# Order of the value matmuls and the side jobs in the second layer's attention of a two-layer transformer kernel

## The chip, the cores and the metric

The kernel runs on one core of one Trainium2 chip. The metric is the time of one execution on the device, in microseconds (us). TensorE, VectorE, ScalarE, GpSimd and SyncE are called PE, DVE, ACT, POOL and SP in the rows, as the profile does.

## What is computed

The input is x, four batches of 1024 tokens of 128 numbers (float32). Two layers are applied, each an attention and a mixture of experts, with a layer norm and a scale and shift ahead of each part. The change touches only the attention of the second layer, layer 1 in the code. It has 16 heads of 8 numbers, in three kinds:

```
outs.append(_sdpa(q[:, :N1], k[:, :N1], v[:, :N1], 1.0 / math.sqrt(HD)))             # 6 heads: softmax(q k)
outs.append(_hyp_attn(q[:, N1:N1 + N2], k[:, N1:N1 + N2], v[:, N1:N1 + N2], curvature))  # 4 heads: hyperbolic
outs.append(_sdpa(qn, kn, v[:, N1 + N2:], math.sqrt(HD)))                            # 6 heads: q and k normalised
```

All are causal. The score of a hyperbolic head is 1 / (eps + arccosh(argument)), where the argument comes from the product of query and key.

## The kernel before

**Batches.** The program goes through the four batches one after the other: layer 0 attention and experts, then layer 1 attention; the experts of layer 1 of a batch run together with the start of the next batch. The engines run separate programs that are tied by semaphores, and a barrier stands between batches.

**Units and steps.** The 16 heads are four units of four heads. Units 0, 1 and 2 of layer 1 are the plain heads (called standard), unit 3 is the hyperbolic one. A unit is cut into 12 steps (`STEPS`): two query chunks of 512 columns, and for each the key blocks of 128 that are not wholly masked. A step has 512, 384, 256 or 128 query columns. Steps 0 to 3 have 512, 384, 256, 128; steps 4 to 8 have 512; steps 9 to 11 have 384, 256, 128.

**Positions.** In layer 1 a loop over positions p (0 to 37) sets the order. With s = p modulo 12, TensorE's program (`tensor_program`, `attention`) does in position p:

1. `scores(p + 1)`: four score matmuls (line 699) in two pairs, one pair into each two-bank buffer. Up to three side jobs are put between them.
2. `values(p)`: the exponentials of step p (tile pr, four heads) against the values vt (line 745). The four heads write 32 partitions each of one PSUM bank, by `tile_position=(0, 32 * j)`, which is 32 columns of the array each. A float32 matmul shows as two instructions, so two heads are x4 in the rows and four heads x8.
3. from p = 6 on `hyp_values(p - 6)`: the value matmuls of two hyperbolic heads (line 772), in the same manner.
4. the side jobs that are left.
5. from p = 3 on `hyp_scores(p - 3)`: two score matmuls (line 715) of hyperbolic heads.

**Side jobs.** Before its own softmax a unit needs the largest score of each query. These are found from a second computation of the scores, cut into pieces: a piece is a matmul of up to 512 columns (line 626), with a mask matmul (line 629) on the diagonal, and a VectorE reduction of its bank (line 1279). The pieces are the side jobs, together with the transposes of the maxima (`max`), of finished outputs (`turn`, line 660) and some work for the next batch. The planner `side_plan` deals them to positions. Side jobs have two PSUM banks, 6 and 7, in turn, and job g waits until VectorE is done with job g - 2:

```
elif g >= 2:
    pe.wait_ge(a.side_out, g - 1)
```

I number the TensorE jobs of a position e0, e1, e2, ... The first three are taken by `scores`; e3 and e4 are the two that the change moves. The number of TensorE jobs in a position, where it is 4 or more, is 11, 5, 10, 9, 8, 6, 9, 7, 6, 4 in positions 0 to 9 and 9, 6, 4, 8, 5, 6, 5, 4, 4 in positions 13 to 21. Positions 10 to 12 and from 22 on have at most three.

**The other engines.** ScalarE does in a position the exponentials of the standard step (line 1008) and, for three hyperbolic half steps in different stages, seven activations: `hyp_exp` (997), `hyp_score` (986, 989, 992), `hyp_root` (980, 981). VectorE does `hyp_arg` (lines 1339, 1344), then the first half of the position's side list, then `hyp_shift` (line 1352), on which ScalarE's next `hyp_exp` depends, then the other half:

```
first = (len(SIDE[l, more][p]) + 1) // 2 if l and k >= 0 else 99
```

(k is p - 3, so this holds from position 3 on; the list counts entries for VectorE alone, such as `maxima`.) GpSimd adds two tiles in `L1616` and masks diagonals. The maxima of the hyperbolic unit go through ScalarE in `hyp_max` (line 967 is its first instruction), at the end of positions 1 and 5. The maxima of unit 1 are formed after position 9 and those of unit 2 after position 21; each goes by a DMA of SP (`send_maxima`) into the query operand before the unit's scores.

Of the kernel before, what the change touches and what calls it, by code (L numbers as in the profile page):

```python
# [53 lines left out]
def diagonals(g):  # L54

    return g // NS * sum(x[4] for x in STEPS) + sum(x[4] for x in STEPS[:g % NS])
# [7 lines left out]
def is_hyp(l, u):  # L64
    return l == 1 and u == HYP_UNIT
# [12 lines left out]
def slot(l, u):  # L78

    return (0, 1, 0, 2)[u] if l else u % SLOTS  # L80
# [16 lines left out]
def nth(l, u):  # L97

    return ((0, 1, 2, 3), (HYP_UNIT, 1, 2))[l].index(u)
# [89 lines left out]
def side_bank(g):  # L189
    return (6, 7)[g % 2]  # L190
# [47 lines left out]
def adaln_kernel(nc, ins, out):  # L238
    with ExitStack() as ctx:
# [105 lines left out]
        def xT(b):  # L345
            return xTs[:, b % 2, :]

        def hT(b):
            return hTs[:, b % 2, :]
# [185 lines left out]
        def chunk(t, c):  # L535
            return t[:, c * CH:(c + 1) * CH]


        def tensor_program(pe, b):
# [18 lines left out]
            def attention(l):  # L558
# [4 lines left out]
                def count(kind, what):  # L563
                    return side_count(l, more, kind, what)
# [44 lines left out]
                def side_job(kind, g, what):  # L609

                    if g == 0:
                        pe.wait_ge(a.v if l == 0 else a.proj_used, NT if l == 0 else 4)
                        if l == 0 and more:
                            pe.wait_ge(fs[1].gates, NC)
                    elif g >= 2:
                        pe.wait_ge(a.side_out, g - 1)
                    bank = side_bank(g)
                    if kind == "piece":
                        u, j, p = what
                        qb, k0, wd, _ = PIECES[p]  # L620
                        if (j, p) == (0, 0):
                            pe.wait_ge(a.ops[u], OPS_HYP if is_hyp(l, u) else OPS)
                        k = K_HYP if is_hyp(l, u) else PAIRS
                        o = ps[:, bank, 0:wd]
                        diag = k0 + wd == (qb + 1) * P
                        mm = pe.matmul(o, qop[0:k, slot(l, u), j, qb * P:(qb + 1) * P],  # L626
                                       kop[0:k, slot(l, u), j, k0:k0 + wd], start=True, stop=not diag)
                        if diag:
                            mm = pe.matmul(o[:, wd - P:wd], identb[:], maskqk[:], start=False, stop=True)  # L629
                    elif kind == "max":  # L630
                        pe.wait_ge(a.nmp, MAXES[l].index(what) + 1)
                        if is_hyp(l, what[0]):
                            mm = pe.transpose(ps[0:32, bank, 0:P], nm[:, nth(l, HYP_UNIT) % 2, :], w["ident"][:])
                        else:
                            mm = pe.matmul(ps[0:96, bank, 0:P], nmp[:], identb[:], start=True, stop=True)
                    elif kind == "out":
                        c = what[0]
                        pe.wait_ge(fs[1].x, c + 1)
                        for t in range(4):
                            mm = pe.transpose(ps[:, bank, t * P:(t + 1) * P],  # L640
                                              xT(b - 1)[:, c * CH + t * P:c * CH + (t + 1) * P], w["ident"][:])
                    elif kind == "xT":
                        c = what[0]
                        pe.wait_ge(x_in, 16)
                        for t in range(4):
                            mm = pe.transpose(ps[:, bank, t * P:(t + 1) * P], xin[:, 4 * c + t, :], w["ident"][:])
                    elif kind == "hT":
                        c = what[0]
                        pe.wait_ge(ln_norm[0], 4 * (c + 1))
                        for t in range(4):  # L650
                            mm = pe.transpose(ps[:, bank, t * P:(t + 1) * P], xin[:, 4 * c + t, :], w["ident"][:])
                    elif kind == "kp":
                        c = what[0]
                        pe.wait_ge(a.side_out, count("hT", (c,)))
                        mm = pe.matmul(ps[:, bank, :], w["wk"][:], chunk(hT(b + 1), c), start=True, stop=True)
                    else:
                        i = what[0]
                        pe.wait_ge(a.o_out, i + 1)
                        for t in range(4):
                            mm = pe.transpose(ps[:, bank, t * P:(t + 1) * P], osb[:, i % 2, t * P:(t + 1) * P],  # L660
                                              w["ident"][:])
                    mm.then_inc(a.side, 1)
# [58 lines left out]
                def out_before(u, c):  # L721

                    same = [i for i, (_, v, d) in enumerate(OUTS[l]) if is_hyp(l, v) == is_hyp(l, u)
                            and (v, d) < (u, c)]
                    return max(same, default=-1) + 1

                def values(g, extra):
                    u, s = divmod(g, NS)
                    c, kb, q0, wd, diag = STEPS[s]
                    o0 = q0 - c * CH  # L730
                    last = kb == 4 * c + 3
                    if diag:
                        pe.wait_ge(a.cut, diagonals(g + 1))
                    else:
                        pe.wait_ge(a.exps, 2 * (g + 1))
                    if kb == 0:
                        if g == 0:
                            pe.wait_ge(a.v, NT if l == 0 else 2)
                        else:
                            pe.wait_ge(a.o_out, out_before(u, c))  # L740
                            if l == 0:
                                pe.wait_ge(a.s_out, NC * u + c)
                    for j in range(4):
                        h = 4 * u + j
                        mm = pe.matmul(ps[32 * j:32 * j + 32, 4, o0:o0 + wd], vt[:, kb, 32 * h:32 * h + 32],  # L745
                                       pr[:, g % 3, j, o0:o0 + wd], start=kb == 0, stop=last,
                                       tile_position=(0, 32 * j))
                        if l and j == 3:
                            mm.then_inc(a.pv, 1)
                        if l and j % 2 and extra:  # L750
                            side_job(*extra.pop(0))
                    if l == 0:
                        for j in range(4):
                            mm = pe.matmul(ps[32 * j:32 * j + 32, 5, o0:o0 + wd], ones32[:],  # L754
                                           pr[:, g % 3, j, o0:o0 + wd], start=kb == 0, stop=last,
                                           tile_position=(0, 32 * j))
                        mm.then_inc(a.pv, 1)
# [18 lines left out]
                def jobs_at(p):  # L776
                    return [x for x in SIDE[l, more][p] if x[1] is not None]
# [9 lines left out]
                for p in range(POSITIONS[l] + 1):  # L787
                    extra = jobs_at(p)
                    if p + 1 < steps:
                        scores(p + 1, extra)  # L790
                    if p < steps:
                        values(p, extra)
                    if l and 0 <= p - HYP_AT - 3 < HYP_HALVES:
                        hyp_values(p - HYP_AT - 3)
                    for x in extra:
                        side_job(*x)
                    if l and 0 <= p - HYP_AT < HYP_HALVES:
                        hyp_scores(p - HYP_AT)
# [1111 lines left out]
```

## Time and profile before

| what | value |
|---|---|
| median of 3 runs | 2942.42 us (2936.65 to 2943.5) |
| the profiled execution | 2944.73 us, its span 2942.8 us |
| PE busy | 2303.2 us, 78% |
| DVE busy | 1553.3 us, 53% |
| ACT busy | 1378.9 us, 47% |
| POOL busy | 657.2 us, 22% |
| mean granted TensorE clock | 0.814 |
| value matmuls, line 745 | 2688 instructions, 442.8 us busy, both layers |

The busy shares are means over stages with different limits. The granted clock is a share of TensorE's full speed of 2.4 GHz: 0.5 stands for the lower level, 1.2 GHz. The attention of layer 1 takes about 276 us of each batch, in the first batch from about 407 to 683 us of the span.

### The profile page before, as it was taken

What the parts mean: (1) busy time and instruction counts of PE and PEld (TensorE: products, weight loads), DVE (VectorE), ACT (ScalarE), POOL (GpSimd) and SP (SyncE); (2) the same over time, 40 slices, a digit from 0 to 9 for tenths busy, and PEclk for the clock granted to TensorE, in tenths of its full rate; (3) what the DMA queues carried; (4) which work ended last, traced back from release to release, by engine and by line L of the source; (5) the groups of instructions that cost most, each with busy time, mean ns of one, the idle gap of its engine ahead of it and who ended that gap; (6) DMA issues with size and microseconds to landing.
All of it is one profiled execution on the core that took longest, in us unless ns stands there. A gap on an engine that the chain in (4) does not pass through costs nothing. (4 is left out here: it accounts for less than half of the span.)

```text
span 2942.8 us, 30130 instructions
## 1 busy us (share of the span) xinstructions
PE 2303.2 (78%) x10649; PEld 866.6 (29%) x10649; DVE 1553.3 (53%) x3429; ACT 1378.9 (47%) x1963; POOL 657.2 (22%) x639
## 2 busy tenths in 40 slices
PE   3799847777999884777798987667789998477789
PEld 1222321223433341122343234121334223212134
DVE  2553446675456354666455526467545634466642
ACT  1145315893134531788224452288622453248932
POOL 1012101332321210233241120033223111013324
PEclk8599866678999885777799987578689998667789
DMA  5100220001400022000330003110032002200012
GB/s 142 40 18 2 73 71 30 17 1 50 128 23 18 16 66 77 27 6 1 95 98 25 2 22 87 50 32 1 12 112 70 18 1 73 67 21 30 1 34 90
DMA packets 67750, 128.32 MB, mean 44 GB/s; under 512 B 11300, under 2 KB 24740, under 8 KB 62980
## 3 DMA queue, kind: packets, MB, share of 16 engines
q1 hardware_dynamic: 67600, 126.40, 14.8%
q8 instruction: 84, 1.38, 0.2%
q14 instruction: 66, 0.54, 0.1%
HBM read 109.99 MB, written 15.20 MB: 43 GB/s over the span
## 5 line engine op out<-in xcount | busy, mean ns | idle before, releaser
L1279 DVE TENSOR_REDUCE mx<-ps 128x1 f32<-128x512 f32 (+3 forms) x1248 | 644.0, 552 | 562.3 <-PE ps L629 468.6
L1008 ACT ACTIVATE pr<-ps 128x1024 f32<-128x1024 f32 (+3 forms) x672 | 515.9, 804 | 537.0 <-PE ps L699 534.4
L626 PE MATMUL ps<-kop,qop 72*128 72x512 bf16 (+6 forms) x1248 | 441.3, 372 | 158.2 <-DVE mx L1279 90.1
L699 PE MATMUL ps<-qop,kop 75*128 75x512 bf16 (+7 forms) x1344 | 409.8, 370 | 160.2 <-DMA kop<-parts_scratch 56.5
L745 PE MATMUL ps<-pr,vt 128*32 128x512 f32 (+3 forms) x2688 | 442.8, 590 | 5.2 <-POOL pr L1563 4.6
L1563 POOL TENSOR_SCALAR_AFFINE_SELECT pr<-pr 128x512 f32<-128x512 f32 x224 | 145.9, 651 | 987.5 <-ACT pr L1008 986.1
L1063 ACT ACTIVATE pr<-ps 128x512 f32<-128x512 f32 x224 | 133.8, 597 | 405.1 <-PE ps L851 316.4
L626 PEld LDWEIGHTS ps<-kop,qop 72*128 72x128 bf16 (+1 forms) x1248 | 124.7, 101 | 608.0 <-DVE mx L1279 342.8
L861 PE MATMUL ps<-pr,w_down 128*128 128x512 f32 x384 | 211.5, 638 | 69.6 <-POOL pr L1554 48.8
L699 PEld LDWEIGHTS ps<-qop,kop 75*128 75x128 bf16 (+1 forms) x1344 | 123.4, 105 | 380.3 <-ACT pr L1008 122.4
L848 PE MATMUL ps<-hT,w_gate 128*128 128x512 f32 x384 | 205.5, 618 | 0.0
L629 PE MATMUL ps<-maskqk,identb 128*128 128x128 bf16 x832 | 200.2, 247 | 0.0
L754 PE MATMUL ps<-pr,ones 128*32 128x512 f32 (+3 forms) x1536 | 166.6, 506 | 0.0
L1329 DVE COPY osb<-ps 128x512 f32<-128x512 f32 x64 | 44.0, 688 | 203.0 <-PE ps L754 176.2
L1554 POOL TENSOR_TENSOR pr<-on,wb 128x512 f32<-128x512 f32 x84 | 106.0, 1264 | 179.6 <-DVE on L1501 129.6
L851 PE MATMUL ps<-hT,w_up 128*128 128x512 f32 x256 | 134.2, 607 | 0.0
L1339 DVE TENSOR_SCALAR wb<-ps 128x1024 f32<-128x1024 f32 (+3 forms) x96 | 91.5, 953 | 72.2 <-PE ps L715 68.0
L1501 DVE TENSOR_TENSOR on<-pr,ps 128x512 f32<-128x512 f32 x84 | 57.3, 682 | 106.9 <-ACT pr L1063 102.3
L861 PEld LDWEIGHTS ps<-pr,w_down 128*128 128x128 f32 x384 | 71.3, 201 | 139.9 <-POOL pr L1554 58.2
L745 PEld LDWEIGHTS ps<-pr,vt 128*32 128x32 f32 x2688 | 69.5, 117 | 133.5 <-issue 108.1
L1616 POOL TENSOR_TENSOR wb<-wb 128x1024 f32<-128x1024 f32 (+3 forms) x36 | 70.9, 1969 | 169.1 <-ACT wb L981 169.1
L715 PE MATMUL ps<-qop,kop 84*128 84x512 bf16 (+3 forms) x192 | 61.8, 414 | 54.4 <-ACT pr L1008 54.4
(298 smaller groups left out, 3012.3 us busy)
## 6 DMA issues: line engine op xcount, KB each, us to landing
wb<-gates_scratch SPq DMA_DIRECT2D x192, 256.0 KB, 3.3
qop<-parts_scratch SPq DMA_DIRECT2D x96, 192.0 KB
kop<-parts_scratch SPq DMA_DIRECT2D x96, 192.0 KB
on<-hmax_scratch SPq DMA_DIRECT2D x8, 1024.0 KB, 5.5
parts_scratch<-on SPq DMA_DIRECT2D x24, 256.0 KB, 3.4
parts_scratch<-wb SPq DMA_DIRECT2D x24, 256.0 KB, 2.9
xin<-in_x SPq DMA_DIRECT2D x4, 512.0 KB, 4.5
on<-in_cos SPq DMA_DIRECT2D x4, 512.0 KB, 3.8
```

The lines of the kernel that those rows point to most:

```text
L626: mm = pe.matmul(o, qop[0:k, slot(l, u), j, qb * P:(qb + 1) * P], kop[0:k, slot(l, u), j, k0:k0 + wd], start=True, stop=not diag)
L629: mm = pe.matmul(o[:, wd - P:wd], identb[:], maskqk[:], start=False, stop=True)
L699: mm = pe.matmul(o, kop[0:k, slot(l, u), 2 * pair + j, kb * P:(kb + 1) * P], qop[0:k, slot(l, u), 2 * pair + j, q0:q0 + wd], start=True, s ...
L745: mm = pe.matmul(ps[32 * j:32 * j + 32, 4, o0:o0 + wd], vt[:, kb, 32 * h:32 * h + 32], pr[:, g % 3, j, o0:o0 + wd], start=kb == 0, stop=la ...
L754: mm = pe.matmul(ps[32 * j:32 * j + 32, 5, o0:o0 + wd], ones32[:], pr[:, g % 3, j, o0:o0 + wd], start=kb == 0, stop=last, tile_position=(0 ...
L848: mm = pe.matmul(ps[:, f.gate_banks[i % R], :], wt, h, start=True, stop=True)
L851: mm = pe.matmul(ps[:, 4 + i % 2, :], wt, h, start=True, stop=True)
L861: pe.matmul(ps[:, c, :], wt, fh[:, i % 3, :], start=i < NC, stop=i == f.last[c]).then_inc(g.down, 1)
L1008: nc.scalar.activation(pr[:, g % 3, 2 * pair:2 * pair + 2, o0:o0 + wd], ps[:, bank:bank + 2, o0:o0 + wd], ACT.Exp).then_inc(a.exps, 1)
L1063: nc.scalar.activation(fa[:, i % 3, :], ps[:, f.gate_banks[i % R], :], fn).then_inc(g.act, 1)
L1279: ins_ = nc.vector.tensor_reduce(mx[:, nth(l, u) % 2, j, qb, col % 2:col % 2 + 1], ps[:, bank, 0:wd], AX.X, ALU.max, negate=True)
L1563: nc.gpsimd.affine_select(past, past, [[0, 4], [1, P]], ALU.is_ge, 0.0, base=0, channel_multiplier=-1).then_inc(at[l].cut, 1)
```

## The change

In `values`, the two lines that put a side job behind the second and the fourth head are gone. The value matmuls of the four heads stand in a row, and the jobs that stood among them are taken by the loop over `extra` behind `hyp_values`, which is unchanged.

```diff
--- before.py
+++ after.py
@@ -747,8 +747,6 @@
                                        tile_position=(0, 32 * j))
                         if l and j == 3:
                             mm.then_inc(a.pv, 1)
-                        if l and j % 2 and extra:
-                            side_job(*extra.pop(0))
                     if l == 0:
                         for j in range(4):
                             mm = pe.matmul(ps[32 * j:32 * j + 32, 5, o0:o0 + wd], ones32[:],
```

The instructions of the other engines, and their order, are the same as before. Lines behind the edit have numbers smaller by two in the changed kernel (772 becomes 770).

TensorE in position 0 of layer 1, from the last score matmul on, before. L745 is `values`, L626 with L629 a piece:

```order
L699 MATMUL ps<-qop,kop 128x384
L626 MATMUL ps<-kop,qop 128x128
L629 MATMUL ps<-maskqk,identb 128x128
L745 MATMUL ps<-pr,vt 32x512 x2
L626 MATMUL ps<-kop,qop 128x128
L629 MATMUL ps<-maskqk,identb 128x128
L745 MATMUL ps<-pr,vt 32x512 x2
L626 MATMUL ps<-kop,qop 128x256
L629 MATMUL ps<-maskqk,identb 128x128
```

The same place with the change:

```order
L699 MATMUL ps<-qop,kop 128x384
L626 MATMUL ps<-kop,qop 128x128
L629 MATMUL ps<-maskqk,identb 128x128
L745 MATMUL ps<-pr,vt 32x512 x4
L626 MATMUL ps<-kop,qop 128x128
L629 MATMUL ps<-maskqk,identb 128x128
L626 MATMUL ps<-kop,qop 128x256
L629 MATMUL ps<-maskqk,identb 128x128
```

The piece e3 now stands behind all four heads, and e4 follows it at once.

TensorE in position 13, from e2 on, before. L772 is `hyp_values`:

```order
L626 MATMUL ps<-kop,qop 128x128
L629 MATMUL ps<-maskqk,identb 128x128
L745 MATMUL ps<-pr,vt 32x384 x2
L626 MATMUL ps<-kop,qop 128x128
L629 MATMUL ps<-maskqk,identb 128x128
L745 MATMUL ps<-pr,vt 32x384 x2
L626 MATMUL ps<-kop,qop 128x256
L629 MATMUL ps<-maskqk,identb 128x128
L772 MATMUL ps<-rsb,vt 32x128 x2
L626 MATMUL ps<-kop,qop 128x256
L629 MATMUL ps<-maskqk,identb 128x128
```

The same place with the change, where L770 is `hyp_values`:

```order
L626 MATMUL ps<-kop,qop 128x128
L629 MATMUL ps<-maskqk,identb 128x128
L745 MATMUL ps<-pr,vt 32x384 x4
L770 MATMUL ps<-rsb,vt 32x128 x2
L626 MATMUL ps<-kop,qop 128x128
L629 MATMUL ps<-maskqk,identb 128x128
L626 MATMUL ps<-kop,qop 128x256
L629 MATMUL ps<-maskqk,identb 128x128
L626 MATMUL ps<-kop,qop 128x256
L629 MATMUL ps<-maskqk,identb 128x128
```

Here e3 and e4 have moved behind `hyp_values` as well.

## Rows read from the trace of the kernel before

**Rows 1.** Windows of the first batch's layer 1: busy us by engine, PEclk.

```profile
434.30:493.90 59.60, 45.75 (x155) 11.83 (x155) 33.78 (x65) 19.62 (x35) 6.60 (x5) 0.59 0.08 29
453.70:467.70 14.00, 13.21 (x51) 4.28 (x52) 8.65 (x18) 3.27 (x5) 1.27 (x2) 0.50 0.20 64
493.90:533.00 39.10, 30.51 (x142) 8.79 (x142) 29.10 (x56) 35.63 (x55) 13.52 (x16) 0.85 0.08 29
582.80:660.00 77.20, 55.08 (x255) 15.65 (x255) 57.67 (x116) 74.87 (x102) 28.11 (x25) 0.81 0.00 1
```

**Rows 2.** Timeline of PE: value matmuls of two heads, and of four.

```profile
588.19 1.05 PE L745 MATMUL ps<-pr,vt 128*32 128x512 f32 x4
589.18 0.28 PE L626 MATMUL ps<-kop,qop 72*128 72x256 bf16 x1
...
670.39 1.07 PE L745 MATMUL ps<-pr,vt 128*32 128x512 f32 x8
```

**Rows 3.** Waits of the whole run: us in total, times, longest.

```profile
PE ps L626 <- DVE mx L1279: 90.1, 201, 1.2
...
ACT nr L967 <- DVE nr L1238: 79.1, 8, 14.3
```

**Rows 4.** Timeline of ACT, first batch: three ends of idle time.

```profile
450.66 0.22 ACT L967 ACTIVATE nr<-nr 128x16 f32<-128x16 f32 x1 [14.30 <-DVE nr L1238]
...
552.95 1.06 ACT L997 ACTIVATE wb<-wb 128x1024 f32<-128x1024 f32 x1 [3.32 <-DVE wb L1352]
...
568.63 1.06 ACT L980 ACTIVATE xn<-xn 128x1024 f32<-128x1024 f32 x1 [1.91 <-DVE xn L1344]
```

**Rows 5.** Timeline of PE, positions 0 and 1: heads 2 and 3.

```profile
437.84 1.92 PE L745 MATMUL ps<-pr,vt 128*32 128x512 f32 x4
439.69 0.40 PE L626 MATMUL ps<-kop,qop 84*128 84x256 bf16 x1
...
447.13 1.50 PE L745 MATMUL ps<-pr,vt 128*32 128x384 f32 x4
```

**Rows 6.** Timeline of PE: position 2's heads 2 and 3; e5 of positions 2 to 4.

```profile
457.41 1.07 PE L745 MATMUL ps<-pr,vt 128*32 128x256 f32 x4
...
458.60 0.32 PE L626 MATMUL ps<-kop,qop 84*128 84x128 bf16 x1
...
465.59 0.42 PE L626 MATMUL ps<-kop,qop 84*128 84x256 bf16 x1
...
477.50 0.42 PE L626 MATMUL ps<-kop,qop 84*128 84x384 bf16 x1
```

**Rows 7.** Timeline of DVE: e3 of positions 2 to 4; position 5 from its shift.

```profile
457.52 0.69 DVE L1279 TENSOR_REDUCE mx<-ps 128x1 f32<-128x512 f32 x1 [0.85 <-PE ps L626]
...
464.82 0.42 DVE L1279 TENSOR_REDUCE mx<-ps 128x1 f32<-128x256 f32 x1 [0.32 <-PE ps L629]
...
475.35 0.56 DVE L1279 TENSOR_REDUCE mx<-ps 128x1 f32<-128x384 f32 x1 [1.83 <-PE ps L629]
...
486.98 1.22 DVE L1352 TENSOR_TENSOR hT<-hT,on 128x1024 f32<-128x1024 f32 x1
488.54 1.29 DVE L1279 TENSOR_REDUCE mx<-ps 128x1 f32<-128x512 f32 x2 [0.34 <-PE ps L629]
```

**Rows 8.** Timeline of PE: positions 9, 13 (two rows) and 14.

```profile
524.93 0.81 PE L772 MATMUL ps<-wb,vt 128*32 128x384 f32 x4
...
549.39 1.49 PE L745 MATMUL ps<-pr,vt 128*32 128x384 f32 x4
...
551.25 0.64 PE L772 MATMUL ps<-rsb,vt 128*32 128x128 f32 x4
...
560.54 1.07 PE L745 MATMUL ps<-pr,vt 128*32 128x256 f32 x4
```

**Rows 9.** Timeline of DVE, position 16: the shift.

```profile
579.66 3.10 DVE L1352 TENSOR_TENSOR xn<-xn,on 128x1024 f32<-128x1024 f32 x1
```

**Rows 10.** Timeline of POOL, position 16.

```profile
579.33 2.35 POOL L1616 TENSOR_TENSOR rsb<-rsb,wb 128x1024 f32<-128x1024 f32 x1 [6.11 <-ACT rsb L981]
```

## Prediction

> **What bounds the kernel now.** I read the windows of the first batch's layer 1 first. They show which engine is full in which stretch, and so where time saved on TensorE is worth anything. From 434.3 to 493.9 us (positions 0 to 5) TensorE is busy 45.75 of 59.6 us and ScalarE only 19.62; from 582.8 to 660.0 (positions 17 and later) ScalarE is busy 74.87 of 77.2 us [rows 1]. So the first stretch runs at TensorE's pace, and in the last one a faster TensorE buys nothing. From 493.9 to 533.0 (positions 6 to 11) ScalarE has 35.63 of 39.1 us, nearly full.
>
> Next the value matmuls. Two heads of 512 columns take 1.05 us, with 0.99 us from their start to the next instruction; four heads in a row take 1.07 us, not 2.1 [rows 2]. The four heads use different columns of the array and run side by side. Two pairs with a job between them pay twice. That is the time the change can take out: the second pair of each position that has four or more side jobs, 19 positions a batch.
>
> Then the waits. TensorE's side jobs wait for VectorE's reductions, 90.1 us in 201 waits, and ScalarE waits 79.1 us in all, in 8 waits (two a batch) for the hyperbolic maxima [rows 3]. The longest in the first batch is 14.30 us, before 450.66 [rows 4]. It ends when the last pieces of position 1 are reduced: whatever TensorE saves before them moves the rest of the layer forward. ScalarE's other idle times in this batch that TensorE can shorten stand in positions 13 and 14: 3.32 and 1.91 us.
>
> **The change, part by part.** No instruction is added or removed; e3 and e4 move. I take the first batch and multiply by four, since the 79.1 us of the waits for the maxima are close to four times its own two.
>
> *Positions 0 and 1: gain 3.3 us.* The second pair of position 0 costs 439.69 - 437.84 = 1.85 us, that of position 1 1.50 less the same 0.07 of overlap, 1.43 [rows 5]. Four heads in a row cost what the first pair costs, by rows 2. After the values the jobs go on as before, only earlier. Both second pairs stand ahead of the last reductions, so the full 3.28 counts.
>
> *Positions 2 to 5: gain 2.9 us.* There the reductions limit it, since with e3 and e4 side by side e5 must wait until e3 is reduced. Position 2: e3's reduction ends at 457.52 + 0.69 = 458.21, and e5 began at 458.60, so the gain is 0.39 at e5 [rows 6, 7]; the second pair is worth 1.00 at most (1.07 less overlap); pieces of 128 columns follow, quick to reduce, and I take 0.6. Position 3: 464.82 + 0.42 = 465.24 against 465.59, 0.35; I take 0.45. Position 4: 475.91 against 477.50, 1.59; two more pieces follow at the reductions' pace of 0.56 each, and I take 1.45. Position 5: `hyp_shift` stays where it was, since e3 is still the last job before it and starts as before. It ends at 488.20, and e4 was reduced from 488.54: 0.34. Sum 2.84. The low bound is 0.39 + 0.35 + (1.59 - 0.56) + 0.34 = 2.1, the high one the pairs themselves, 1.00 + 0.45 + 1.85 + 1.85 = 5.2 (for positions 4 and 5, of 512 columns, I take position 0's).
>
> *Positions 6 to 9: loss 0.8 us.* Now `hyp_values` stands ahead of e3 and e4. In position 6, e4 is the last job before the shift; it gains one pair and loses one `hyp_values` of the same cost, nothing; I book 0.1 lost. In position 7 e3 is the last, and comes later by one pair, 0.98; see below why I book only 0.1. In position 9 e3 is the last piece but none before unit 1's maxima, and nothing may start on unit 1 until these are sent. It comes later by the 0.81 us of `hyp_values` less 0.07 [rows 8], part of which VectorE's shift covered; I book 0.6. In position 8 the shift does not depend on e3 or e4. TensorE's own saving in these positions meets a full ScalarE, so I cost it at nothing; that cover is gone where ScalarE idles, and there is some of that in the other batches.
>
> *Positions 13 and 14: gain 1.7 us.* In 13, e4 is again the last before the shift. It gains the pair, 1.49 - 0.07 = 1.42, and pays `hyp_values` of 128 columns, 0.57: 0.85 net, and ScalarE waits there 3.32 us on that shift [rows 4, 8]. In 14 the shift is untouched, but `hyp_scores` come earlier by the pair, 1.00, less the wait for e3's reduction ahead of the last job, 0.15; ScalarE waits 1.91 us for their result. I take 0.85.
>
> *Positions 15 to 21: loss 0.2 us.* In 16, e3 is the last before the shift and comes about 1.05 us later. But there the shift took 3.10 us, where others of its shape take 1.22 [rows 7, 9]. It began 0.33 us after GpSimd's addition, which ran until 579.33 + 2.35 = 581.68, and ended at 582.76 [rows 10]. Started a microsecond later it still ends about there: nothing lost. Position 7 has the same pattern. Without this cover positions 7 and 16 would lose 2.0 us more a batch, 8 in all, and the time would be 2923. The Trainium skill (SBUF — State Buffer, "Who interferes with whom") says that a VectorE instruction with two SBUF inputs is blocked for the whole length of a GpSimd instruction that reads SBUF. The 3.10 us agree. In 21, unit 2's maxima come later by part of a `hyp_values`; behind the same kind of cover, 0.2.
>
> *Sum.* 3.28 + 2.84 + 1.70 - 0.8 - 0.2 = 6.8 us a batch, 27 in all. The profiled execution took 2944.7, which gives 2917.5; the median of the runs is 2.3 lower, so 2915. With positions 2 to 5 at 2.1 and positions 7 and 16 uncovered it is 4.1 a batch, 2926; with positions 2 to 5 at 5.2 it is 9.2, 2906.
>
> **The rivals.**
>
> *The reductions set the pace everywhere.* The Trainium skill (TensorEngine Tiling (Array Packing), "PSUM Bottleneck") warns that a faster, packed TensorE may leave the PSUM evacuation as the bottleneck. Here that would mean: only positions 0 and 1 gain, 3.3 less 1.0 lost, 9 us in all, 2933. For it speaks position 5, where 0.34 of 1.85 is left. Against it, VectorE is busy only 33.78 of 59.6 us there [rows 1]. The sum by my rows is 2915, by that rule 2933. Chance 0.10.
>
> *The clock is lost.* Positions 0 to 5 have a mean granted clock of 0.59, which is 18% of 59.6 us, 10.7 us, at 2.4 GHz and the rest at 1.2 [rows 1]. If the denser order brings less of the higher level, TensorE's work of these 10.7 us takes up to twice as long; some 7 of it would be on the path, which takes the whole gain: 2942. For it speaks that 13.21 busy us of 14 were not enough for the higher level between 453.7 and 467.7 (0.50). Against it: no work is taken out. Chance 0.06.
>
> *The clock is won.* The same stretch at 2.4 GHz would take TensorE half of 13.2 us, and VectorE's 8.65 would bind it: up to 5 us a batch more, 2895. Chance 0.08.
>
> *Slower: the shift is held up.* e3 and e4 stand behind `hyp_values` in 13 positions (6 to 9, 13 to 21). If in each of them VectorE's shift had to wait for them, ScalarE's full stretch would grow by a `hyp_values` each time, 13 x 1.0 = 13 us a batch against a gain of 6.1 in positions 0 to 5: 7 lost a batch, 28 in all, 2970. It decides from about seven such positions on. Against it speaks the rule for the first half of the list: only in positions 6, 7, 13 and 16, with lists of 7 to 9 entries, does that half reach e3 or e4; in the others it holds three at most. For it: a late e3 holds e5 and with it `hyp_scores`, and the full ScalarE has little slack. Chance 0.10.
>
> **How the numbers follow.** My forecast has 0.66. Two runs of this kernel differ by some 0.2%, so 0.3%, 9 us, is what a measurement can tell from no change. Faster by more than that: the forecast, the clock won and half of the first rival, 0.79. Within: the other half and the clock lost, 0.11. Slower: 0.10. The range goes from 2894, the clock won, to 2939, behind the first rival; it leaves out the slower case, the lost clock and a few in a hundred beyond the low end.
>
> **What would show it.** The value matmuls of positions 0 to 21 stand as x8 of 1.07 us (about 1.9 at the lower clock), none as x4. The first batch's wait before line 967 falls from 14.30 to about 11.0. The stretch from the first piece of position 0 to the second `hyp_max` is shorter by about 6 us, and the stretch from position 17 on has the same length, with ScalarE full. The shifts of positions 7 and 16 end as late after GpSimd's addition as before. It is wrong if the wait at 552.95 grows, if the x8 groups take twice 1.05, or if positions 15 to 22 grow by more than a microsecond.

## The result, and the profile after

The changed kernel takes 2927.27 us (median of 4 runs, 2924.84 to 2929.63), the kernel before on the same chip 2942.96 (4 runs, 2936.65 to 2946.84). The ratio is 0.9949, with an interval of 0.9929 to 0.9968. A second comparison, with more runs, stands among the experiments: 0.997 [0.9953, 0.9987]. So the change makes the kernel faster by 0.3 to 0.5% (the two intervals reach from 0.1 to 0.7%). That is inside the range, on the side that was forecast, and smaller: 16 us by the first comparison and 7 by the second, where 27 were forecast.

The page of the changed kernel, its busy times and the group of value matmuls (busy us, mean ns of one):

```profile
PE 2286.9 (78%) x10649; PEld 872.5 (30%) x10649; DVE 1541.9 (53%) x3429; ACT 1379.5 (47%) x1963; POOL 656.4 (22%) x639
...
L745 PE MATMUL ps<-pr,vt 128*32 128x512 f32 (+3 forms) x2688 | 361.7, 617 | 5.2 <-POOL pr L1561 4.7
```

The value matmuls take 361.7 us where they took 442.8, 81 less. All of TensorE is busy only 16 us less: its other instructions took 65 us longer, and its mean granted clock went from 0.814 to 0.790.

The wait for the hyperbolic maxima, which the first term rested on, fell as forecast. A wait of the changed kernel (us in total, times, longest), then ScalarE's timeline in the first batch:

```profile
ACT nr L965 <- DVE nr L1236: 65.8, 8, 11.7
```

```profile
447.48 0.22 ACT L965 ACTIVATE nr<-nr 128x16 f32<-128x16 f32 x1 [10.77 <-DVE nr L1236]
...
508.64 0.84 ACT L995 ACTIVATE rsb<-rsb 128x768 f32<-128x768 f32 x1 [2.39 <-DVE rsb L1350]
...
551.16 1.06 ACT L995 ACTIVATE wb<-wb 128x1024 f32<-128x1024 f32 x1 [2.64 <-DVE wb L1350]
...
565.91 1.06 ACT L978 ACTIVATE xn<-xn 128x1024 f32<-128x1024 f32 x1 [0.97 <-DVE xn L1342]
...
580.12 1.06 ACT L995 ACTIVATE xn<-xn 128x1024 f32<-128x1024 f32 x1 [1.76 <-DVE xn L1350]
```

Against [rows 4]: 14.30 became 10.77 (11.0 forecast), 3.32 became 2.64 and 1.91 became 0.97. But the second line is new. ScalarE waits 2.39 us for the shift of position 7, where the kernel before had:

```profile
512.98 0.84 ACT L997 ACTIVATE rsb<-rsb 128x768 f32<-128x768 f32 x1 [0.92 <-DVE rsb L1352]
...
582.80 1.06 ACT L997 ACTIVATE xn<-xn 128x1024 f32<-128x1024 f32 x1 [1.72 <-DVE xn L1352]
```

**Where the time went.** I cut each batch's layer 1 at marks on ScalarE: the first instruction of each `hyp_max`, then the score activation (line 984, 986 before) of positions 9, 11, 16, 18, 22 and 28. Lengths in us; where one number stands, it is the mean of the four batches' gains.

| stretch | before, batches 1 to 4 | changed | mean gain | forecast |
|---|---|---|---|---|
| first piece of position 0 to first `hyp_max` | 16.37, 15.44, 16.37, 16.38 | 12.84, 13.77, 12.78, 12.95 | 3.06 | 3.28 |
| to the second `hyp_max` (positions 2 to 5) | 39.83, 38.44, 39.79, 39.80 | 37.21, 37.22, 37.21, 37.20 | 2.25 | 2.84 |
| to position 9 (positions 6 to 8) | 29.57, 31.90, 29.58, 29.58 | 31.04, 31.63, 31.13, 30.90 | -1.02 | -0.2 |
| 9 to 11 | 9.84, 10.34, 9.83, 9.83 | 12.89, 10.59, 10.54, 12.90 | -1.77 | -0.6 |
| 11 to 16 | 43.54, 43.29, 43.39, 42.14 | 42.09, 41.05, 41.42, 42.00 | 1.45 | 1.7 |
| 16 to 18 | 18.96, 19.16, 19.15, 18.18 | 19.20, 19.86, 19.86, 19.20 | -0.67 | -0.2, to 21 |
| 18 to 22 | 33.6, 35.4, 35.4, 34.4 | 33.6, 33.6, 33.6, 33.6 | 1.1 | 0 |

From position 22 to 28 every batch has the same length as before to 0.01 us. The rows add to 4.4 us a batch, 18 in all; the profiled span is shorter by 2942.8 - 2927.9 = 14.9, so some 3 us were lost elsewhere. Most of the missing time is in positions 6 to 11: 0.8 booked as lost, 2.8 measured. The windows of the changed kernel for the stretches of [rows 1] (busy us by engine, then PEclk, DMA share, GB/s), then for positions 9 to 11 of the four batches:

```profile
434.64:488.18 53.54, 39.21 (x156) 11.10 (x156) 33.67 (x65) 19.70 (x35) 6.62 (x5) 0.56 0.10 32
488.18:532.00 43.82, 35.55 (x142) 10.22 (x142) 27.51 (x56) 36.00 (x54) 13.09 (x16) 0.62 0.07 25
580.20:657.50 77.30, 57.33 (x255) 17.56 (x255) 58.29 (x116) 74.82 (x102) 28.46 (x25) 0.69 0.00 1
...
515.73:528.62 12.89, 9.90 (x50) 3.29 (x48) 9.39 (x22) 9.41 (x19) 4.09 (x7) 0.63 0.01 2
1221.99:1232.58 10.59, 6.54 (x47) 2.49 (x47) 9.19 (x22) 9.32 (x19) 4.12 (x7) 0.91 0.00 1
1928.64:1939.18 10.54, 6.58 (x47) 2.49 (x47) 9.14 (x22) 9.31 (x19) 4.11 (x7) 0.91 0.00 1
2635.55:2648.45 12.90, 9.95 (x50) 3.24 (x48) 9.39 (x22) 9.42 (x20) 4.10 (x7) 0.63 0.00 1
```

The first stretch lost 6.5 us of TensorE work and 6.1 us of length. The second, of positions 6 to 11, grew from 39.1 to 43.8 and its clock fell from 0.85 to 0.62. The last kept its length with ScalarE full, although its clock fell too, from 0.81 to 0.69. The last four rows are one order of instructions in four batches: two batches had a clock of 0.91 and took 10.5 us, two had 0.63 and took 12.9. The kernel before had 0.95 and 9.84 in the first batch:

```profile
520.06:529.90 9.84, 6.60 (x47) 2.27 (x44) 8.43 (x20) 9.21 (x19) 4.13 (x7) 0.95 0.01 3
```

**Position 7, where the new wait is.** TensorE before and after:

```profile
509.05 1.05 PE L745 MATMUL ps<-pr,vt 128*32 128x512 f32 x4
510.04 0.23 PE L626 MATMUL ps<-kop,qop 72*128 72x128 bf16 x1
...
510.25 1.05 PE L745 MATMUL ps<-pr,vt 128*32 128x512 f32 x4
```

```profile
503.56 1.94 PE L745 MATMUL ps<-pr,vt 128*32 128x512 f32 x8
505.28 1.92 PE L770 MATMUL ps<-xn,vt 128*32 128x512 f32 x4
507.13 0.23 PE L626 MATMUL ps<-kop,qop 72*128 72x128 bf16 x1
```

VectorE in the changed kernel:

```profile
507.45 0.29 DVE L1277 TENSOR_REDUCE mx<-ps 128x1 f32<-128x128 f32 x1 [3.10 <-PE ps L629]
507.66 0.95 DVE L1350 TENSOR_TENSOR rsb<-rsb,on 128x768 f32<-128x768 f32 x1
```

e3 used to come 1 us behind the start of the values. Now it stands behind `values` and `hyp_values`, and both take 1.9 us each at the lower clock: 3.57 us. VectorE waits 3.10 us for it, and the shift that ScalarE needs stands behind that reduction in VectorE's list.

In batches 1, 3 and 4 this one wait is all that positions 6 to 8 lost: they grew by 1.47, 1.55 and 1.32 us, and ScalarE's wait for this shift grew from 0.92 or 0.93 to 2.39, 2.48 and 2.24.

Two things are mixed here, the order and the clock. They call for these theories: **order** (a job that the first half of VectorE's list reaches holds the shift, so it is cured by moving e3 and e4 or by shortening the list), **clock alone** (the lower clock came by itself and the order is innocent), and **too little work on the array** (grouping empties TensorE, and that is why the clock falls).

### The profile page after: what moved, and what is told of

It reads as the page before. It is cut to its first block and busy times, and to the rows that moved or that the text cites. A ratio compares the mean times of both kernels' runs of the same rounds, so it can differ in the third digit from the quotient of the medians.

```text
span 2927.9 us, 30130 instructions
## 1 busy us (share of the span) xinstructions
PE 2286.9 (78%) x10649; PEld 872.5 (30%) x10649; DVE 1541.9 (53%) x3429; ACT 1379.5 (47%) x1963; POOL 656.4 (22%) x639
## 5 line engine op out<-in xcount | busy, mean ns | idle before, releaser
L626 PE MATMUL ps<-kop,qop 72*128 72x512 bf16 (+6 forms) x1248 | 457.8, 389 | 160.2 <-DVE mx L1277 93.7
L699 PE MATMUL ps<-qop,kop 75*128 75x512 bf16 (+7 forms) x1344 | 428.2, 384 | 150.9 <-DMA kop<-parts_scratch 56.3
L745 PE MATMUL ps<-pr,vt 128*32 128x512 f32 (+3 forms) x2688 | 361.7, 617 | 5.2 <-POOL pr L1561 4.7
L626 PEld LDWEIGHTS ps<-kop,qop 72*128 72x128 bf16 (+1 forms) x1248 | 126.1, 103 | 568.2 <-DVE mx L1277 319.7
L629 PE MATMUL ps<-maskqk,identb 128*128 128x128 bf16 x832 | 203.7, 252 | 0.0
L846 PEld LDWEIGHTS ps<-hT,w_gate 128*128 128x128 f32 x384 | 75.1, 199 | 91.8 <-issue 75.0
```

The source lines that it names most:

```text
L699: mm = pe.matmul(o, kop[0:k, slot(l, u), 2 * pair + j, kb * P:(kb + 1) * P], qop[0:k, slot(l, u), 2 * pair + j, q0:q0 + wd], start=True, s ...
L846: mm = pe.matmul(ps[:, f.gate_banks[i % R], :], wt, h, start=True, stop=True)
```

## Experiments

Each kernel is the changed one with the edit shown, unless said otherwise. Each of the three sets ran on a chip of its own, so I compare by the ratio to the kernel before on the same chip. That kernel had 2940.99, 2941.84 and 2939.37 us there, from 23 to 29 runs.

### Set 1: where the gain is made, and e3 and e4 moved back ahead

Grouped in positions 0 to 5 only:

```diff
+                        if l and g >= 6 and j % 2 and extra:
+                            side_job(*extra.pop(0))
```

> The four value matmuls are grouped only in positions 0 to 5 of layer 1; from position 6 on e3 and e4 stand among them as in the kernel before. Theory A (the lower granted clock in positions 6 to 12 comes from the grouping there, and ate most of the gain): the gain of positions 0 to 5 stays, 6.1 us a batch, 24 in all, and the granted clock between position 6 and 12 is again about 0.85; time 2918 to 2921. Theory B (the clock level there is chance, or follows from the earlier positions): the clock stays at 0.62 there and the time is 2925 to 2930, like the changed kernel.

Measured: 2932.68 us, 0.9971 [0.9947, 0.9996]. Faster, by 8 us where the forecast's terms for 0 to 5 come to 24. Neither theory's range holds the time. Its profiled execution took 2956.46 us, 24 above its own median, so its trace can only hint. Positions 0 to 5 took 49.9 to 51.0 us there, as in the changed kernel. Positions 6 to 8, where the jobs stand as before, took 30.9, 30.0, 30.0 and 30.2 us at clocks of 0.70 to 0.75; three batches of the kernel before had 29.6 at 0.83. So a part of the loss behind position 5 may come from what the grouping of positions 0 to 5 leaves behind. That is not shown.

Grouped from position 6 on only (the same lines with `g < 6`):

> The complement: grouped only from position 6 on. Theory A: the gain of positions 0 to 5 is gone and the loss of positions 6 to 12 (4 us in the first batch) stands against some 3 us gained in positions 13 to 19: time 2942 to 2950, clock in positions 6 to 12 about 0.62. Theory B: clock there back at 0.85 and time 2935 to 2939.

Measured: 2936.06, 0.9988 [0.997, 1.0005], not told from no change, and within theory B's range. But the clock in positions 6 to 8 was 0.62 to 0.72, so theory B's clock did not come with it. Gains and losses from position 6 on about cancel. Its first stretch, which is ungrouped as before, took 16.1, 13.2, 13.3 and 12.9 us in the four batches, at clocks of 0.61, 0.85, 0.84 and 0.87. Grouped, the same stretch took 12.95 us at 0.63 in the changed kernel's fourth batch, and 11.6 at 0.79 in two batches of its second trace (changed_again). So the gain depends on the clock: about 3.4 us at the lower one, and some 1.3 to 1.7 at the higher one.

e3 and e4 ahead of `hyp_values`, in all positions:

```diff
+                    for x in extra[:2]:
+                        side_job(*x)
+                    extra = extra[2:]
                     if l and 0 <= p - HYP_AT - 3 < HYP_HALVES:
                         hyp_values(p - HYP_AT - 3)
```

> Grouped everywhere, but e3 and e4 stand behind the four value matmuls and ahead of the hyperbolic ones. Theory C (the loss in positions 6 to 12 comes from e3 and e4 waiting behind the hyperbolic value matmuls, which delays VectorE's shift): the loss goes, time 2912 to 2918. Theory A: the clock stays at about 0.62 in positions 6 to 12 and only the part of the shift waits in positions 7 and 9 comes back, 1 to 2 us a batch: time 2920 to 2925.

Measured: 2903.54 (2886.04 to 2911.74), 0.9881 [0.9853, 0.9908], more than either theory expected. The values stay grouped, and the gain is over twice that of the change.

The same with e3 alone (`extra[:1]`):

> Grouped everywhere; e3 stands behind the four value matmuls, then the hyperbolic ones, then e4. The side jobs break the run of value matmuls once instead of not at all. Theory C: 2912 to 2918. Theory A: if a break between the two groups is what keeps the clock up, the clock in positions 6 to 12 is near 0.85 and the time 2915 to 2920; if the total of column passes side by side matters, it stays near 0.62 and the time is 2920 to 2925.

Measured: 2917.27, 0.9941 [0.9919, 0.9963]. That is clearly less than with both ahead, so e4 counts too. It is the last job before the shift in positions 6 and 13. The interval overlaps that of the changed kernel in set 2.

### Set 2: only where the shift waits, everywhere, and more work on the array

The changed kernel again, as the measure for this set:

> The changed kernel once more, on the same chip as the next three, so that they are compared with it directly. 2922 to 2930 us; in positions 9 to 11 it is slower than before wherever the granted clock there is near 0.65 and not near 1.

Measured: 2934.36 (2922.26 to 2944.15, 12 runs), 0.997 [0.9953, 0.9987], 4 us above the expected range. Its trace repeats the loss: positions 6 to 8 took 31.7, 31.1, 31.7 and 30.9 us, with a wait for the shift of position 7 of 2.1 to 2.5 us in each batch. Positions 9 to 11 took 12.2 to 12.9 us in all four batches, at clocks of 0.60 to 0.63.

e3 and e4 ahead only in the four positions where the first half of VectorE's list reaches them:

```diff
+                    if l and p in (6, 7, 13, 16):
+                        for x in extra[:2]:
+                            side_job(*x)
+                        extra = extra[2:]
```

> e3 and e4 ahead of the hyperbolic value matmuls only in positions 6, 7, 13 and 16, where the first half of VectorE's list reaches them. If VectorE's shift is what they hold up, most of what the kernel with both ahead everywhere gains over the changed one comes back (6 us a batch by the traces): 2904 to 2910. If they hold up something else (the side ring, the maxima, the hyperbolic scores), it stays near 2920 to 2927.

Measured: 2904.5 (2882.99 to 2914.34), 0.9886 [0.9865, 0.9908], as good as moving them in all positions. This bears out the order theory: what costs is that the shift waits, and in four positions. The wait for the shift of position 7 is 0.91 or 0.92 us in every batch of this kernel, as before the change. Positions 6 to 8 of the first batch, changed and shift_only:

```profile
484.69:515.73 31.04, 23.86 (x89) 6.50 (x90) 17.32 (x34) 26.49 (x39) 7.30 (x8) 0.61 0.10 35
```

```profile
482.17:510.53 28.36, 19.80 (x98) 6.25 (x98) 20.25 (x37) 26.50 (x38) 8.93 (x8) 0.79 0.12 38
...
510.53:519.88 9.35, 5.98 (x41) 1.99 (x40) 7.59 (x19) 9.16 (x20) 3.60 (x7) 0.89 0.01 3
1204.55:1216.85 12.30, 8.95 (x48) 3.01 (x47) 9.20 (x21) 9.42 (x20) 4.11 (x7) 0.61 0.00 1
```

The stretch is 2.7 us shorter, and its clock is 0.79, not 0.61. The order works at an equal mean clock too. Positions 6 to 8 took 28.1 us at 0.70 here in the second batch and 27.5 at 0.69 in the fourth batch of list_three (below), but 31.2 at 0.69 in the fourth batch of ahead_13_16, which has the changed order there.

The last two rows are positions 9 to 11, whose order this edit leaves as in the changed kernel: 9.35 us in one batch at 0.89 and 12.30 in the next at 0.61. The order within the stretch does not explain this difference. Nor does its mean clock by itself. Here are two batches of list_three, again with the changed kernel's order in positions 9 to 11:

```profile
510.53:521.23 10.70, 7.77 (x40) 2.45 (x40) 7.09 (x19) 9.30 (x20) 3.79 (x7) 0.57 0.01 2
...
2612.91:2625.80 12.89, 9.96 (x50) 3.33 (x48) 9.39 (x22) 9.42 (x20) 4.08 (x7) 0.63 0.00 1
```

The batch with the lower clock is 2.2 us shorter. Between the same two marks of ScalarE, TensorE has 40 instructions to do there and 50 in the other: it came into the stretch further ahead. And in e3_ahead, where e3 stands ahead in positions 8 and 9 as well, two batches took 9.33 and 9.35 us at 0.59. So what is carried in from position 8 counts beside the clock, and the trace does not part the two.

All side jobs that are left ahead of `hyp_values` (its call moved behind the loop over `extra`):

> Grouped, and all side jobs that are left stand ahead of the hyperbolic value matmuls. If every side job that is earlier helps: a few us below the kernel with both ahead, 2895 to 2903. If the hyperbolic value matmuls between e4 and e5 are useful cover for the reductions: no better, 2903 to 2912.

Measured: 2943.36, 1.0004 [0.9988, 1.002]; the whole gain is gone, and the time lies far above both expected ranges. ScalarE and VectorE of its first batch:

```profile
502.61 0.84 ACT L978 ACTIVATE wb<-wb 128x768 f32<-128x768 f32 x1 [2.08 <-DVE wb L1342]
...
604.73 1.06 ACT L978 ACTIVATE hT<-hT 128x1024 f32<-128x1024 f32 x1 [1.57 <-DVE hT L1342]
```

```profile
500.62 0.96 DVE L1337 TENSOR_SCALAR wb<-ps 128x768 f32<-128x768 f32 x1 [1.90 <-PE ps L715]
```

`hyp_values` (1 to 1.9 us) now stand directly ahead of `hyp_scores` (line 715), and VectorE's `hyp_arg` and then ScalarE wait for these. The second row lies past position 17, where ScalarE had no such wait in the first batch of before and of changed. That `hyp_values` had cost nothing between the side jobs, because TensorE waits for a reduction there anyway, is my reading and not tested. The clock in positions 6 to 8 was 0.50 in this batch, so the clock has a part here as well.

The score matmuls of positions 5 to 11 doubled, 28 more instructions a batch (each writes the same product again):

```diff
+                            for _ in range(2 if l and 6 <= g < 13 else 1):
+                                mm = pe.matmul(o, kop[0:k, slot(l, u), 2 * pair + j, kb * P:(kb + 1) * P],
+                                               qop[0:k, slot(l, u), 2 * pair + j, q0:q0 + wd], start=True, stop=True)
```

> The changed kernel with every score matmul of steps 6 to 12 of layer 1 issued twice, to the same result: 28 more matmuls a batch of up to 512 columns, 0.22 us each at the high clock and 0.43 at the low one. If the low clock in positions 6 to 12 comes from too little work on the array, the clock there goes from 0.62 to 0.85 or more and positions 8 to 11 take 1 to 3 us less a batch: time 2915 to 2927 in spite of the added work. If not: clock as before and 4 to 8 us more a batch, 2940 to 2955.

Measured: 2952.64, 1.0038 [1.0022, 1.0054]. Positions 6 to 8 of the first and the third batch:

```profile
485.95:519.70 33.75, 27.34 (x100) 8.84 (x100) 17.55 (x34) 26.49 (x39) 7.43 (x8) 0.60 0.10 32
1910.07:1940.01 29.94, 22.40 (x100) 7.58 (x100) 17.84 (x34) 26.49 (x38) 8.11 (x8) 0.73 0.11 36
```

With TensorE busy 27.3 us of 33.8 the clock stays at 0.60, and so it does in the second and fourth batch. The third has 0.73, with TensorE busy 22.4 us of 29.9, so less. The added work did not raise the clock, and the theory of too little work on the array has nothing left that speaks for it.

### Set 3: the two pairs of positions apart, and the cure on VectorE

Ahead in positions 6 and 7 only:

> Grouped; e3 and e4 ahead of the hyperbolic value matmuls in positions 6 and 7 only. Theory S (they hold up VectorE's shift where its first half reaches them): positions 6 to 8 take 1.2 us less than before instead of 1.4 more, positions 13 to 16 as in the changed kernel; 2.7 us a batch and, if the low clock in positions 9 to 11 is a consequence of the delay in 6 and 7, up to 3 us more: time 2912 to 2918. If the clock there is independent of it: 2918 to 2924.

Measured: 2912.07, 0.991 [0.9877, 0.9943]. Positions 6 to 8 took 28.1, 30.3, 28.3 and 28.6 us, where the changed kernel had 30.9 to 31.6.

Ahead in positions 13 and 16 only:

> The same in positions 13 and 16 only. Theory S: positions 13 to 16 take 3 us less a batch than in the changed kernel, positions 6 to 11 as there, with the clock in 9 to 11 at 0.63 to 0.73: time 2916 to 2922. The two gains together should make up the 25 to 30 us between the changed kernel and the one with all four positions.

Measured: 2928.7 (2903.82 to 2943.52), 0.9954 [0.9927, 0.9982], above the expected range and not told from the changed kernel. From the score activation of position 14 to that of 18 the batches took 37.60, 37.54, 37.55 and 34.58 us, the changed kernel 37.5 to 37.8 in its first trace (36.5 in two batches of its second). The fourth has a clock of 0.80, the first 0.60:

```profile
548.42:586.02 37.60, 31.13 (x118) 9.32 (x117) 29.49 (x47) 32.92 (x38) 10.87 (x5) 0.60 0.00 1
...
2680.00:2714.58 34.58, 25.09 (x122) 7.57 (x120) 28.88 (x48) 32.77 (x38) 10.81 (x5) 0.80 0.00 1
```

Position 16 shows a threshold. Here are VectorE, GpSimd and ScalarE of its first batch:

```profile
573.48 2.85 DVE L1354 TENSOR_TENSOR xn<-xn,on 128x1024 f32<-128x1024 f32 x1
...
572.90 2.35 POOL L1618 TENSOR_TENSOR rsb<-rsb,wb 128x1024 f32<-128x1024 f32 x1 [6.12 <-ACT rsb L983]
...
576.36 1.06 ACT L999 ACTIVATE xn<-xn 128x1024 f32<-128x1024 f32 x1 [1.71 <-DVE xn L1354]
```

And the same three in shift_only:

```profile
566.67 1.22 DVE L1354 TENSOR_TENSOR xn<-xn,on 128x1024 f32<-128x1024 f32 x1
...
567.40 2.70 POOL L1618 TENSOR_TENSOR rsb<-rsb,wb 128x1024 f32<-128x1024 f32 x1 [6.12 <-ACT rsb L983]
...
569.04 1.06 ACT L999 ACTIVATE xn<-xn 128x1024 f32<-128x1024 f32 x1
```

In ahead_13_16 the shift starts 0.58 us behind GpSimd's addition, takes 2.85 us and ScalarE waits 1.71, as in the kernel before (1.72). In shift_only it starts 0.73 us ahead of the addition, takes 1.22, and ScalarE has no idle time there; the addition takes 2.70 in place of 2.35. An earlier e3 brings nothing until it is early enough to come first. In batches 1 to 3 of ahead_13_16 the shift starts 0.56 to 0.58 us behind the addition; in the fourth it starts 0.73 us ahead, and only there is the stretch 3 us shorter. How close the race can be, other places show: a shift of the same shape that started 0.07 us ahead of an addition took 1.22 us (shift_only, position 6), and one that started 0.07 us behind took 3.36 (list_three, position 13, third batch).

The cure on VectorE: the changed TensorE program, but from position 6 on the shift stands behind at most three entries of its list.

```diff
                     first = (len(SIDE[l, more][p]) + 1) // 2 if l and k >= 0 else 99
+                    if l and k >= 3:
+                        first = min(first, 3)
```

> The changed kernel on TensorE; on VectorE, from position 6 on, at most three side jobs stand ahead of the shift, so that it never waits for e3 or e4. Theory S: the loss goes without any change on TensorE, 2900 to 2915. If the place of e3 and e4 costs through the side ring or the score buffers: 2922 to 2935.

Measured: 2898.66 (2889.49 to 2905.84), 0.9851 [0.9816, 0.9886]. This is just below the range that was expected, and the lowest ratio of all kernels, clearly below before and changed; both_ahead and shift_only have intervals that overlap it. It is the most direct test of the order theory, since TensorE's program stays the changed one. VectorE in position 7:

```profile
501.30 0.94 DVE L1350 TENSOR_TENSOR rsb<-rsb,on 128x768 f32<-128x768 f32 x1
502.73 0.49 DVE L1277 TENSOR_REDUCE mx<-ps 128x1 f32<-128x128 f32 x2 [0.50 <-PE ps L629]
```

The shift starts ahead of e3's reduction, and ScalarE's activation behind it follows at 503.45 with no wait, where the changed kernel had 2.39.

The same VectorE edit on the kernel before:

> The kernel before (pairs with jobs among them) with the same shorter first half on VectorE. Shows what of that gain has nothing to do with the grouping: theory S expects some gain, since e4 of positions 6 and 13 and e3 of 7 and 16 stand ahead of the shift there too, one or two pairs later than they might: 2925 to 2938.

Measured: 2932.32, 0.998 [0.9958, 1.0002]. Without the grouping the short list brings 7 us, with an interval that reaches no change; with it, about 1% or 30 us against the changed kernel (0.9851 against 0.9949 and 0.997). The two edits need each other: the grouping makes e3 and e4 late, the list makes that harmless. The traces show why the list alone brings little. In the first batch of before_list_three ScalarE's wait for the shift of position 7 is gone too, but it waits 1.34 us for `hyp_arg` just ahead, and in positions 16 to 18 2.25 us. With the grouping these waits are 0.62 and 0.59 us.

## Why the prediction was right, and too large

- *Positions 0 and 1, 3.28.* Right: 3.5 us in the three batches whose clock was as in the rows read, 1.67 in the second, which was quicker before (15.44 us, at a clock of 0.69 and not 0.60) and slower after (13.77, at 0.50). Scaling the first batch by four missed that.
- *Positions 2 to 5, 2.84.* Right: 2.6 in three batches, 1.22 in the second. The bounds of 2.1 and 5.2 held for the three. The reductions took most of what four pairs could give, as rows 6 and 7 showed.
- *Positions 6 to 9, a loss of 0.8.* This step failed: 2.8 us lost on average, up to 4.5 (batches 1 and 4). It failed in two terms.
  - Positions 6 to 8 lost 1.3 to 1.6 us in three batches, and all of it is the wait for the shift of position 7, which was booked at 0.1, on the ground that GpSimd's addition covered it. The changed trace shows the shift at 507.66 us, taking 0.95, no longer behind a lock (2.37 us before) but behind e3. The cover was 1.4 us long, and the delay of e3 2.6 (from 0.99 to 3.57 us behind the start of the values). I had priced `values` and `hyp_values` at the 1.0 us of the higher clock, which rows of the same stretch showed at 0.85; at the lower one each costs 1.9.
  - Positions 9 to 11 lost 3.05 us in batches 1 and 4 and 0.25 and 0.71 in the others, where 0.6 was booked because unit 1's maxima come later. That was the wrong wait: in these two traces ScalarE never waits for unit 1's first scores. In the first batch it waits for VectorE's `hyp_arg` (1.15 and 1.16 us) and for a shift (0.96), 3.27 us in all against 0.44 before:

```profile
519.38 0.63 ACT L978 ACTIVATE hT<-hT 128x512 f32<-128x512 f32 x1 [1.15 <-DVE hT L1342]
...
526.80 0.42 ACT L978 ACTIVATE xn<-xn 128x256 f32<-128x256 f32 x1 [1.16 <-DVE xn L1342]
```

- *Positions 13 and 14, 1.7.* Nearly right: ScalarE's two waits fell by 0.68 and 0.94, and the stretch from 11 to 16 by 1.45 on average.
- *Positions 15 to 21, a loss of 0.2.* The cover in position 16 held in the way that was forecast, in three batches of four. In the first the shift began at 578.87 us, as GpSimd's addition ended (576.61 + 2.35 = 578.96), and ScalarE waited 1.76 us where it had waited 1.72:

```profile
578.87 1.22 DVE L1350 TENSOR_TENSOR xn<-xn,on 128x1024 f32<-128x1024 f32 x1
...
576.61 2.35 POOL L1614 TENSOR_TENSOR rsb<-rsb,wb 128x1024 f32<-128x1024 f32 x1 [6.11 <-ACT rsb L979]
```

  In the fourth batch there had been no cover. The kernel before had its shift 0.74 us ahead of the addition there, and ScalarE did not wait; with the change it waits 1.76 us. The first batch alone could not show this.

```profile
2713.95 1.21 DVE L1352 TENSOR_TENSOR xn<-xn,on 128x1024 f32<-128x1024 f32 x1
...
2714.69 2.68 POOL L1616 TENSOR_TENSOR rsb<-rsb,wb 128x1024 f32<-128x1024 f32 x1 [6.12 <-ACT rsb L981]
```

- *What the rows say of the lock.* A shift that starts 0.58 us behind GpSimd's instruction takes 2.85 us, one 0.73 us ahead of it 1.22, and then GpSimd's takes 2.70 in place of 2.35. The Trainium skill (SBUF — State Buffer, "Who interferes with whom") says that the order of issue decides who blocks. The trace agrees in both cases.
- *Positions 16 to 21 as measured.* In the stretch behind position 16 there were 0.67 us of loss, and in positions 18 to 21 of the other three batches 0.9 to 1.9 us of gain, since ScalarE had idled there before and no longer does; I had costed these at nothing. That gain is luck for the forecast: without its 1.1 us a batch the rows would add to 3.3 and not to 4.4. The second trace of the changed kernel has it in part only (34.7, 34.2, 34.7 and 33.6 us from 18 to 22).
- *The rivals.* "The reductions set the pace everywhere" does not hold: positions 2 to 5 gained 2.25 us, where that rival gives none, and positions 13 and 14 gained too. The Trainium skill (TensorEngine Tiling (Array Packing), "PSUM Bottleneck") says only that the copy out of PSUM may become the bottleneck; in this trace it did not, save in position 5 as the prediction read it. "The clock is lost" and "the shift is held up" were each partly true, but the loss came in positions 6 to 11, and from both together. In positions 2 to 5 the clock did fall, from 0.58 to 0.64 before to 0.50 to 0.52, and the stretch still became 2.25 us shorter. Kept apart, each rival had too small a chance; the text named positions 7 and 16 as places of the held shift and booked both as covered. The 8 us set aside for the case without cover would have brought the time near the result, but only partly for the right reason: position 16 was covered in three batches, and the loss of positions 9 to 11 is not in them.

**What stays open.** Why the clock is lower in positions 6 to 11 of the changed kernel. It did not rise when work was added (doubled_scores: 0.60 in three batches, 0.73 in one). Order plays a part: with the shift cured (shift_only), positions 6 to 8 have 0.79, 0.70, 0.80 and 0.79. But positions 9 to 11 show 0.61 and 0.89 in two batches of one kernel. Nor is it shown what part of the loss follows from quicker positions 0 to 5: in the second batch of the kernel before, positions 2 to 5 took 38.4 us in place of 39.8, and positions 6 to 8 31.9 in place of 29.6. All medians hold both kinds of batch, and runs of one kernel differ by up to 1.4% (2903.82 to 2943.52). So the order is shown by the comparisons of medians and by the waits of each batch, and the share of the clock in the medians is not measured.

## What to carry to other kernels

When instructions are grouped on one engine, look at what they are put ahead of: list for every moved job who consumes it, and what stands behind that consumer on its own in-order engine. Here the grouping alone brought 0.3 to 0.5%, and shortening the consumer's list ahead of its critical instruction made it 1.5%; neither edit did that alone. Price moved work at both clock levels that the trace shows, not at the one of the stretch as it was. Look at each batch and not at the first alone: the fourth had no cover in position 16. And do not take a stretch's mean clock for the cause of its length before its waits are read.

## What had not been expected of the hardware

- One order of instructions ran at granted clocks of 0.63 and 0.91 in two batches of one execution, and took 12.9 and 10.5 us; in another kernel the same order took 10.7 us at 0.57. Doubling TensorE's score matmuls left the clock at 0.60 in three batches of four.
- The contention of VectorE and GpSimd is a threshold in time: a shift 0.07 us ahead of the addition took 1.22 us, one 0.07 us behind it 3.36.
- 81 us less of busy time in the value matmuls went with only 16 us less of TensorE busy time in all, the mean clock being 0.790 in place of 0.814.
